# Starting addresses of the supports, the attention output and the transposed x3 in a four-block graph kernel

## The chip, the cores and the metric

The kernel runs on one core of a Trainium2 chip. The metric is the device time of one execution in microseconds, and the figure given is the median of three runs. The engines are named as the profile names them: PE is TensorE (its matmuls), PEld is TensorE's loading of the stationary operand, DVE is VectorE, ACT is ScalarE, POOL is GpSimd and SP is SyncE, which issues the transfers.

## The reference

There are 32 graphs of 256 nodes with 256 features, and a 256 x 256 weighted adjacency each. Every graph passes four blocks, each a residual with a layer norm behind it:

```
x = layernorm(x + relu([x, adj@x / deg] @ W.T))                        # block 0
x = layernorm(x + gcn3(x))          # h = relu(adj@(x@W1)+b1); h = relu(adj@(h@W2)+b2); adj@(h@W3)+b3
x = layernorm(x + attention(x))     # 8 heads of 64, softmax*0.33 + 0.33*adj + 0.33*exp(-adj), then @W_out + b_out
x = layernorm(x + gate(x))          # w = softmax over nodes of sum_m(q@k.T * adj)/8, times v
```

All is float32, and the results are float32.

## The kernel before

The work is written out by hand for each engine, with semaphores between them. One graph takes 340 matmul records on PE, and in the steady part a `slot(s)` runs steps of up to six graphs in turn: the gate of an old one, the attention of a younger one, the three graph-convolution layers of the next, block 0 of the newest. The slots are the loop around everything that the change touches. Nothing but the order of calls in `slot` sets the order on an engine.

**Split products.** To keep float32 precision, every operand of the big products is held as two float32r tiles, a high part (suffix `_h`, written by ACT with `copy`, line 378) and a low part (suffix `_l`, the rest, written by DVE, line 830). A product then takes three passes: high x high, low x high, high x low. `product` (line 1478 holds its matmul) runs them, and each matmul has its own load of a 128 x 128 stationary block (`left`); the moving operand (`right`) is 256, 384 or 512 columns wide. So each matmul is a pair: a weight load of 128 columns from one SBUF address, and a stream of columns from another. The load for the next pair is done while the present one streams. In the profile's names, `psum<-A,B` has the moving operand A first and the stationary B second.

**Steps around the change**, by the names of the tiles:
- The supports `sup` (x times W, before the adjacency is applied). In `hidden` (layers 0 and 1) `sup` is stationary and the adjacency `adjT` is moving; in `gcn_out` and `aggregate` it is the other way round. Each of the four has 12 matmuls of 256 columns per graph.
- `project_out`: `oT`, the attention output, is stationary, and `wout` is moving: 24 matmuls of 256 columns.
- `tail_project`: `x3T` is stationary, `w3` is moving: 12 matmuls of 384 columns.
- `tail_adj_k`: the adjacency is stationary and `k3` (in the profile `k`) is moving, 128 or 64 columns: 8 matmuls.

**Where the tiles lie.** Tiles are allocated in the order of their declarations, each from the next multiple of 32 bytes. Nearly all of them are multiples of 128 bytes long, so a position modulo 128 bytes is carried on from tile to tile, and the little tiles named `space_0`, `space_1` and `space_2` (and the tail `HALF` in the rows of `qkT`) only shift what comes behind them. Every block that a matmul reads starts a multiple of 128 bytes behind its tile's start (in `qkT` a multiple of 64), so the position of the tile is that of all its blocks. Before the change, modulo 128: all weights (`w0`, `w123`, `wqkv`, `wout`, `w3`) at 32; `adjT`, `fT`, `hidT`, `x2T`, `oT`, `x3T`, `k3`, `v_sb`, `x1`, `x2`, `x3` at 96; `sup` at 32; `ident` at 64; `work` at 0. So the stationary and the moving operand of every split product are 64 bytes apart, but for `k3` and the adjacency, which are 0 apart.

Of the kernel before, what the change touches and what calls it, by code (L numbers as in the profile page):

```python
# [7 lines left out]
F32R = mybir.dt.float32r  # L8
# [5 lines left out]
def graph_blocks_kernel(nc, x, adj, nodemask, xT, adjT_in, L0_WT, L1_W1, L1_b1, L1_W2, L1_b2, L1_W3, L1_b3,  # L14
                        L2_Wqkv, L2_Wout, L2_bout, L3_WT, out):
    G, N, F = x.shape
    P = 128
    NT = N // P
# [11 lines left out]
    HALF = 16  # L30
# [7 lines left out]
    with ctx:  # L38
        def sb(name, shape, dt=F32):
            return ctx.enter_context(nc.sbuf_tensor(name, shape, dt))  # L40
# [45 lines left out]
        adjT = [sb(f"adjT_{s}", [P, ADJS, NT, N], F32R) for s in "hl"]  # L86
        fT = [sb(f"fT_{s}", [P, FT, N], F32R) for s in "hl"]

        sb("space_0", [P, HALF])
        sup = [sb(f"sup_{s}", [P, NT, F], F32R) for s in "hl"]  # L90
        sb("space_1", [P, HALF])
        self_part = sb("self_part", [P, NT, F])
        x1_pre = sb("x1_pre", [P, NT, F])
        x1 = sb("x1", [P, NT, F])
# [14 lines left out]
        psum_exp = sb("psum_exp", [P, 2, 2, NT])  # L109
        rsum = sb("rsum", [P, 2, 2, NT])  # L110
        probT = work[:, 1].rearrange("p (a h j i) -> p a h j i", a=2, h=2, j=NT)
        sb("space_2", [P, HALF // 2])
        oT = [sb(f"oT_{s}", [P, PAIRS, N], F32R) for s in "hl"]
        x3_pre = sb("x3_pre", [P, NT, F])
        x3 = sb("x3", [P, NT, F])
# [47 lines left out]
        def bank(n):  # L163
            return psum[:, n]
# [44 lines left out]
        def once(g):  # L209
            return min(g + 1, G)  # L210

        def nth(g, p):
            return min(PAIRS * g + p + 1, PAIRS * G)

        def nth2(g, p, i):
            return min(2 * (PAIRS * g + p) + i + 1, 2 * PAIRS * G)

        def live(g):
            return 0 <= g < G
# [4 lines left out]
        def reuse(eng, semaphore, n):  # L224

            if n > 0:
                eng.wait_ge(semaphore, n)
# [1237 lines left out]
        def _(pe):  # L1465
# [9 lines left out]
            def product(dst, terms, passes=ALL, opens=True, closes=True):  # L1475
                steps = [(left[a], right[b]) for left, right in terms for a, b in passes]
                for n, (left, right) in enumerate(steps):
                    last = mm(dst, left, right, start=opens and n == 0, stop=closes and n == len(steps) - 1)  # L1478
                return last

            def cut(parts, *index):
                return [a[index] for a in parts]
# [3 lines left out]
            def block_of(i, size=P):  # L1486
                return slice(i * size, (i + 1) * size)

            def transpose_tiles(dst, src):
                for r in range(2):  # L1490
                    for t in range(2):
                        last = nc.tensor.transpose(dst[:, r * N + t * P:r * N + (t + 1) * P],  # L1492
                                                   src[:, t, block_of(r)], ident[:, :])
                return last
# [14 lines left out]
            def weights(g, number):  # L1509
                if g == 0:  # L1510
                    pe.wait_ge(dve_w, number)
# [135 lines left out]
            def qk(g, p):  # L1647
                if not live(g):
                    return
                weights(g, W_QKV + 1)  # L1650
                pe.wait_ge(dve_x2T, once(g))
                if p in (2, 3):
                    reuse(pe, act_oT, nth(g - 1, p))
                    reuse(pe, dve_oT, nth(g - 1, p))
                if p == 1:
                    reuse(pe, dve_oT, nth(g - 1, p - 1))
                if p == 0:
                    pe.wait_ge(act_x2T, once(g))
                if p == 3:
                    pe.wait_ge(dve_sup0, once(g + 2))  # L1660
                    pe.wait_ge(act_sup0, once(g + 2))
                for i in range(2):
                    last = product(bank(QK[p])[:, i * N:(i + 1) * N],
                                   [(cut(wqkv, A, k, i, block_of(p)), cut(x2T, A, k)) for k in range(FT)])
                last.then_inc(pe_qk, 1)
# [23 lines left out]
            def probs_t(g, p, h):  # L1689
                if not live(g):  # L1690
                    return
                if (p, h, g) == (0, 0, 31):
                    pe.wait_ge(dve_prob, nth2(g, 0, 0))
                else:
                    pe.wait_ge(dve_prob, nth2(g, p, h))
                    if p == 0 and h == 1:
                        pe.wait_ge(dve_qk, nth(g, p + 2))
                        pe.wait_ge(act_qk, nth(g, p + 2))
                    if p == 1 and h == 1:
                        pe.wait_ge(act_probT, nth2(g, p - 1, 0))  # L1700
                    if p == 2 and h == 1:
                        pe.wait_ge(act_qk, nth(g + 1, p - 2))
                        pe.wait_ge(dve_qk, nth(g + 1, p - 2))
                    if p == 0 and h == 0:
                        pe.wait_ge(act_v, once(g))
                    if p == 3 and h == 1:
                        reuse(pe, act_qkv3, once(g - 1))
                transpose_tiles(bank(PROBT[p][h]), prob[:, p % 2, :, h]).then_inc(pe_probT, 1)
# [79 lines left out]
            def gate_column(g):  # L1788
                if not live(g):
                    return  # L1790
                pe.wait_ge(dve_gate_prob, once(g))
                pe.wait_ge(dve_x2_pre, once(g + 3))
                pe.wait_ge(act_gate_exp, once(g))
                for t in range(NT):
                    last = nc.tensor.transpose(bank(GATE_COL)[:, t:t + 1], gate_prob[:, block_of(t)], one[:, :])  # L1795
                last.then_inc(pe_gate_col, 1)

            def slot(s):
                hidden(0, s - 2, HI)
                tail_adj_k(s - 5)  # L1800
                hidden(0, s - 2, LO)
                probs_t(s - 4, 2, 0)
                probs_t(s - 4, 2, 1)
                probs_t(s - 4, 3, 0)
                probs_t(s - 4, 3, 1)
                scores(s - 3, 0)
# [4 lines left out]
                support(1, s - 2, HI)  # L1811
                support(1, s - 2, LO)
                qk(s - 3, 2)
                support0(s - 1, HI)
                hidden(1, s - 2, HI)
# [11 lines left out]
                aggregate(s - 1, HI)  # L1827
                aggregate(s - 1, LO)
                qk(s - 3, 3)
                gate_column(s - 5)  # L1830
                probs_t(s - 3, 0, 0)
                probs_t(s - 3, 0, 1)
# [7 lines left out]
                x3_transpose(s - 4)  # L1840
                x1_transpose(s - 1)
                qk(s - 2, 0)
                tail_project(s - 4, HI)
                support(0, s - 1, HI)
# [124 lines left out]
            def last_graphs():  # L1969
# [24 lines left out]
                values(G - 2, LO)  # L1994
                qk(G - 2, 3)
                gate_column(G - 4)
                probs_t(G - 2, 0, 0)
                probs_t(G - 2, 0, 1)
# [24 lines left out]
                project_out(G - 2, HI)  # L2023
                project_out(G - 2, LO)
                gate_column(G - 3)
                probs_t(G - 1, 0, 0)
                probs_t(G - 1, 0, 1)
# [70 lines left out]
```

## Time and profile before

| | us |
|---|---|
| median of 3 runs | 1299.63 (1298.72 to 1299.93) |
| the profiled execution, its own time | 1296.4 |
| its span | 1294.6 |
| PE busy / share of span | 1276.8 / 99% |
| DVE busy / share of span | 1198.8 / 93% |
| ACT busy / share of span | 912.2 / 70% |

The busy time of PE counts every moment in which some matmul is under way. A matmul of 256 columns stands in the trace with about 280 ns, but the next one starts about 115 ns after it; what a matmul costs a busy PE is this distance between starts, and it is read from the timeline as the difference between the start of one row and that of a later one, divided by the matmuls between them. The time outside the span is 1.8 us in the profiled execution.

### The profile page before, as it was taken

The page shows a single profiled execution, that of the slowest core. Times are in us where ns is not written, and L with a number is a line of the kernel's source. Part 1 is how long each engine was busy: PE and PEld are TensorE (multiplying, and loading weights), DVE is VectorE, ACT ScalarE, POOL GpSimd, SP SyncE. Part 2 cuts the span into 40 slices and gives each one's busy share as a digit, 9 for nine tenths or more (in the row PEclk, how much of TensorE's full clock was granted, in tenths as well). Part 3 has the DMA queues.
Part 4 walks back from the last instruction along what each step waited for, and adds up shares of the span by engine and source line. Part 5 has one row for each costly group of instructions (what it writes and reads, how often), then busy time and mean ns, then how long its engine had stood idle before and what let it go on. Part 6 is the DMA issues. An engine that isn't in the chain of part 4 may idle for free.

```text
span 1294.6 us, 30579 instructions
## 1 busy us (share of the span) xinstructions
PE 1276.8 (99%) x10987; PEld 1173.4 (91%) x10987; DVE 1198.8 (93%) x3821; ACT 912.2 (70%) x2445; POOL 139.7 (11%) x265
## 2 busy tenths in 40 slices
PE   8999999999999999999999999999999999999997
PEld 7899999999999999999999999999999999999985
DVE  6898999999999999999999999999999999998996
ACT  6677767677667677677677676776676776776773
POOL 0000110101110101111101101011101011110011
PEclk9999999999999999999999999999999999999999
DMA  5211011110111110111100111101111101110000
GB/s 193 68 35 35 1 44 43 43 43 2 43 43 43 43 36 8 43 43 43 43 20 25 44 43 43 43 2 43 43 43 43 35 10 43 43 43 10 9 10 25
DMA packets 51588, 49.03 MB, mean 38 GB/s; under 512 B 7920, under 2 KB 51184, under 8 KB 51440
## 3 DMA queue, kind: packets, MB, share of 16 engines
q1 hardware_dynamic: 51440, 47.08, 11.7%
q8 instruction: 90, 1.47, 0.5%
q14 instruction: 58, 0.48, 0.1%
HBM read 38.68 MB, written 8.39 MB: 36 GB/s over the span
## 4 chain that ended last, share of the span: by engine, by line
PE 96%; DVE 1%; ACT 1%; DMA 1%; issue 0%; POOL 0%; SPq 0%; POOLq 0%; DVEq 0%; ACTq 0%
PE psum L1478 63%; PE psum L1492 13%; PE psum L1722 9%; PE psum L1684 8%; PE psum L1773 1%; PE psum L1776 1%; DMA adj_sb<-in_adj 1%; PE psum L1785 1%; PE psum L1795 0%; POOL rstd L338 0%; ACT fT_h L378 0%; DVE bn L859 0%; SPq L238 0%; DVE x L893 0%; ACT adj_junk L434 0%
## 5 line engine op out<-in xcount | busy, mean ns | idle before, releaser
L526 ACT ACTIVATE work<-work,shift 128x256 f32<-128x256 f32 x512 | 253.6, 499 | 35.9 <-DVE shift L1022 35.9
L1041 DVE SCALAR_TENSOR_TENSOR work<-work,rsum,extra 128x256 f32<-128x256 f32 x512 | 216.4, 472 | 0.2
L378 ACT ACTIVATE work<-psum 128x512 f32<-128x512 f32 x256 | 138.2, 595 | 76.1 <-PE psum L1492 72.2
L1022 DVE CUSTOM_DVE_ANT_0 work<-psum,minus_big 128x256 f32<-128x256 f32 x512 | 189.3, 415 | 0.7 <-PE psum L1684 0.7
L378 ACT ACTIVATE sup_h<-psum 128x512 fp32r<-128x512 f32 x128 | 75.9, 593 | 148.0 <-PE psum L1478 148.0
L335 POOL TENSOR_TENSOR mv<-mv,eps 128x2 f32<-128x2 f32 x128 | 33.0, 258 | 1140.8 <-DVE mv L880 1140.8
L1478 PE MATMUL psum<-x2T_h,wqkv_h 128*128 128x256 f32 x512 | 145.3, 284 | 0.0
L1478 PE MATMUL psum<-x2T_l,wqkv_h 128*128 128x256 f32 x512 | 142.2, 278 | 0.0
L1478 PE MATMUL psum<-x2T_h,wqkv_l 128*128 128x256 f32 x512 | 142.1, 278 | 0.0
L1492 PE MATMUL psum<-ident,work 128*128 128x128 f32 x1024 | 129.3, 274 | 0.0
L1722 PE MATMUL psum<-work,v_sb 128*64 128x256 f32 x1024 | 124.6, 385 | 0.0
L1492 PEld LDWEIGHTS psum<-ident,work 128*128 128x128 f32 x1024 | 112.8, 141 | 1.3 <-issue 0.4
L378 ACT ACTIVATE qkT_h<-psum 128x512 fp32r<-128x512 f32 x128 | 75.5, 591 | 50.9 <-PE psum L1478 50.9
L338 POOL TENSOR_TENSOR rstd<-mv,minus_half 128x2 f32<-128x2 f32 x128 | 107.0, 836 | 10.0
L1722 PEld LDWEIGHTS psum<-work,v_sb 128*64 128x64 f32 x1024 | 67.8, 136 | 36.5 <-issue 0.2
L526 ACT ACTIVATION_READ_ACCUMULATOR work<-work,shift 128x1 f32 x512 | 97.2, 190 | 0.0
L1478 PE MATMUL psum<-w_h,fT_h 128*128 128x256 f32 x384 | 93.7, 280 | 3.2 <-ACT fT_h L378 2.1
L1478 PEld LDWEIGHTS psum<-x2T_l,wqkv_h 128*128 128x128 f32 x512 | 96.7, 189 | 0.1
L1478 PEld LDWEIGHTS psum<-x2T_h,wqkv_h 128*128 128x128 f32 x512 | 96.2, 188 | 0.5 <-issue 0.2
L1478 PEld LDWEIGHTS psum<-x2T_h,wqkv_l 128*128 128x128 f32 x512 | 96.1, 188 | 0.0
L859 DVE BATCH_NORM_STATS2 bn<-x_pre 128x6 f32<-128x256 f32 x256 | 94.5, 410 | 0.2
L1478 PE MATMUL psum<-w_l,fT_h 128*128 128x256 f32 x384 | 93.1, 278 | 0.0
(134 smaller groups left out, 3735.2 us busy)
## 6 DMA issues: line engine op xcount, KB each, us to landing
xT_sb<-in_xT SPq DMA_DIRECT2D x32, 256.0 KB, 2.8
adjT_sb<-in_adjT SPq DMA_DIRECT2D x32, 256.0 KB, 3.2
adj_sb<-in_adj SPq DMA_DIRECT2D x32, 256.0 KB, 4.7
x_sb<-in_x SPq DMA_DIRECT2D x32, 256.0 KB, 4.9
out<-y_sb SPq DMA_DIRECT2D x32, 256.0 KB, 4.6
work<-in_L_gnn_W_qkv SPq DMA_DIRECT2D x1, 1536.0 KB, 9.6
mask_row<-in_nodemask SPq DMA_DIRECT2D x32, 32.0 KB, 4.6
w_raw<-in_L_gnn_W SPq DMA_DIRECT2D x3, 256.0 KB, 6.7
```

What stands on the lines that cost most here:

```text
L335: nc.gpsimd.tensor_tensor(mv[:, k, :, 1], mv[:, k, :, 1], eps[:, :], ALU.add) \
L338: nc.gpsimd.tensor_tensor(rstd[:, k], mv[:, k, :, 1], minus_half[:, :], ALU.pow) \
L378: return nc.scalar.activation(dst, src, ACT.Copy, scale=scale)
L526: last = nc.scalar.activation(prob[:, p % 2, i, h], prob[:, p % 2, i, h], ACT.Exp, bias=shift[:, p % 2, h, i:i + 1], scale=-1.0, accum_out ...
L859: last = V_.bn_stats(out=bn[:, k, t], in_=src[:, t])
L1022: last = V_.tensor_tensor_reduce(out=prob[:, p % 2, i, h], in0=bank(SCORES[p] + h)[:, i * N:(i + 1) * N], in1=minus_big[:, g % 2, i], scal ...
L1041: last = V_.scalar_tensor_tensor(out=prob[:, p % 2, i, h], in0=prob[:, p % 2, i, h], scalar=rsum[:, p % 2, h, i:i + 1], in1=extra[:, g % 2 ...
L1478: last = mm(dst, left, right, start=opens and n == 0, stop=closes and n == len(steps) - 1)
L1492: last = nc.tensor.transpose(dst[:, r * N + t * P:r * N + (t + 1) * P], src[:, t, block_of(r)], ident[:, :])
L1684: last = mm(bank(SCORES[p] + h)[:, i * N:(i + 1) * N], qkT[left][rows, p % 2, 0, block_of(i)], qkT[right][rows, p % 2, 1], start=n == 0 an ...
L1722: last = mm(bank(PV[p])[h * D:(h + 1) * D, 0:N], v_sb[:, k, (2 * p + h) * D:(2 * p + h + 1) * D], probT[:, p % 2, h, k], start=k == 0, sto ...
L1773: mm(bank(ADJK)[:, at:at + 2 * D], adjT[0][:, g % ADJS, k, block_of(t)], k3[:, k].rearrange("p a d -> p (a d)"), start=k == 0, stop=False)
```

## The change

It alters where four groups of tiles start, and nothing of what is computed or in which order:
- `space_0` shrinks from 64 to 32 bytes, each support tile gets 16 bytes of padding at its start, and `space_1` shrinks likewise. `sup_h` then starts at 16 modulo 128 and `sup_l` at 48, where both were at 32. Against `adjT` at 96 they are 48 and 80 bytes apart, where both were 64. All from `self_part` on stays where it was.
- `space_2` grows from 32 to 64 bytes. All tiles behind it move on by 32 bytes: `oT`, `x3_pre`, `x3`, `x3T`, `qkv3`, `k3`, `gate` go from 96 to 0 modulo 128, and the small tiles, `x4_pre`, `y_sb`, `bn`, `mv` and `rstd` with them. `oT` and `x3T` are then 96 bytes behind their weights (which are at 32) where they were 64, and the adjacency 96 behind `k3` where it was 0.
- At three places two of PE's waits for semaphores that stand next to each other (in the third with one between) change places. The same semaphores and values are waited for before the same matmul.

```diff
-        sb("space_0", [P, HALF])
-        sup = [sb(f"sup_{s}", [P, NT, F], F32R) for s in "hl"]
-        sb("space_1", [P, HALF])
+        sb("space_0", [P, 8])
+        sup = [sb(f"sup_{s}", [P, 4 + NT * F], F32R)[:, 4:].rearrange("p (t f) -> p t f", t=NT) for s in "hl"]
+        sb("space_1", [P, 8])
...
-        sb("space_2", [P, HALF // 2])
+        sb("space_2", [P, 16])
         oT = [sb(f"oT_{s}", [P, PAIRS, N], F32R) for s in "hl"]
...
                 if p == 3:
+                    pe.wait_ge(act_sup0, once(g + 2))
                     pe.wait_ge(dve_sup0, once(g + 2))
-                    pe.wait_ge(act_sup0, once(g + 2))
...
                     if p == 0 and h == 1:
+                        pe.wait_ge(act_qk, nth(g, p + 2))
                         pe.wait_ge(dve_qk, nth(g, p + 2))
-                        pe.wait_ge(act_qk, nth(g, p + 2))
...
                 pe.wait_ge(dve_gate_prob, once(g))
+                pe.wait_ge(act_gate_exp, once(g))
                 pe.wait_ge(dve_x2_pre, once(g + 3))
-                pe.wait_ge(act_gate_exp, once(g))
```

Every engine's list of instructions, without its waits, is the same before and after.

## Rows read from the trace of the kernel before

**Rows 1.** Page: span, busy time and share of each engine, granted clock
```profile
span 1294.6 us, 30579 instructions
...
PE 1276.8 (99%) x10987; PEld 1173.4 (91%) x10987; DVE 1198.8 (93%) x3821; ACT 912.2 (70%) x2445; POOL 139.7 (11%) x265
...
PEclk9999999999999999999999999999999999999999
```
**Rows 2.** Page: the chain that ended last, by engine
```profile
PE 96%; DVE 1%; ACT 1%; DMA 1%; issue 0%; POOL 0%; SPq 0%; POOLq 0%; DVEq 0%; ACTq 0%
```
**Rows 3.** Windows of one slot each: busy us of each engine, records, clock, transfers
```profile
605.00:644.28 39.28, 39.28 (x342) 36.26 (x342) 37.10 (x121) 28.19 (x77) 4.38 (x8) 1.00 0.12 35
900.00:939.28 39.28, 39.28 (x345) 36.25 (x343) 37.10 (x120) 28.19 (x77) 4.38 (x8) 1.00 0.12 36
```
**Rows 4.** PE's waits: for whom, us in total, times, longest
```profile
PE psum L1478 <- ACT sup_h L378: 2.5, 5, 1.1
...
PE psum L1478 <- ACT x3T_h L378: 0.4, 1, 0.4
```
**Rows 5.** Timeline of PE, 590 to 604 us: start, us, operation, count
```profile
591.58 0.28 PE L1478 MATMUL psum<-w_h,fT_h 128*128 128x256 f32 x1
...
592.52 0.28 PE L1478 MATMUL psum<-adjT_h,sup_h 128*128 128x256 f32 x1
...
593.94 0.63 PE L1478 MATMUL psum<-w_h,fT_l 128*128 128x256 f32 x4
...
595.77 0.28 PE L1478 MATMUL psum<-wout_h,oT_h 128*128 128x256 f32 x1
...
598.49 0.28 PE L1478 MATMUL psum<-w_h,hidT_h 128*128 128x256 f32 x1
...
599.85 0.39 PE L1478 MATMUL psum<-wqkv_h,x2T_h 128*128 128x512 f32 x1
...
601.68 0.28 PE L1478 MATMUL psum<-sup_h,adjT_h 128*128 128x256 f32 x1
...
603.04 1.10 PE L1478 MATMUL psum<-wqkv_h,x2T_l 128*128 128x512 f32 x4
```
**Rows 6.** The same timeline, 604 to 619 us
```profile
604.12 0.28 PE L1478 MATMUL psum<-sup_h,adjT_l 128*128 128x256 f32 x1
...
605.41 0.28 PE L1478 MATMUL psum<-x2T_h,wqkv_h 128*128 128x256 f32 x1
...
615.45 0.34 PE L1478 MATMUL psum<-w_l,x3T_h 128*128 128x384 f32 x1
...
616.69 0.28 PE L1478 MATMUL psum<-w_h,fT_h 128*128 128x256 f32 x1
...
618.07 0.85 PE L1478 MATMUL psum<-w_h,x3T_l 128*128 128x384 f32 x4
618.76 0.28 PE L1478 MATMUL psum<-x2T_h,wqkv_h 128*128 128x256 f32 x1
```
**Rows 7.** The same timeline, 620 to 624 us
```profile
620.17 0.28 PE L1478 MATMUL psum<-adjT_h,sup_h 128*128 128x256 f32 x1
...
621.12 0.34 PE L1773 MATMUL psum<-k,adjT_h 128*128 128x128 f32 x2
...
621.93 0.72 PE L1478 MATMUL psum<-adjT_h,sup_l 128*128 128x256 f32 x4
622.49 1.91 PE L1492 MATMUL psum<-ident,work 128*128 128x128 f32 x16
```
**Rows 8.** Page: a group by line: count, busy us, mean ns, idle before
```profile
L1492 PE MATMUL psum<-ident,work 128*128 128x128 f32 x1024 | 129.3, 274 | 0.0
```
**Rows 9.** Groups of DVE by line: count, busy us, mean ns, idle before
```profile
L830 DVE TENSOR_TENSOR sup_l<-psum,sup_h 128x512 fp32r<-128x512 f32 x128 | 87.4, 682 | 2.4 <-ACT sup_h L378 2.4
...
L830 DVE TENSOR_TENSOR x2T_l<-psum,x2T_h 128x512 fp32r<-128x512 f32 x32 | 21.8, 682 | 0.0
```

## The prediction

> **What bounds the kernel now.** I read the page's first part first. PE is busy for 99% of the span, DVE for 93%, and PE's clock is granted in full, so at the higher of its levels, 2.4 GHz, all the way [rows 1]. The chain of waits says the same: 96% of it is PE, with no other engine over 1% [rows 2]. The windows of two steady slots, each 39.28 us, show PE busy for all 39.28 us and DVE for 37.10 [rows 3]. PE's waits are a few in the whole run: 2.5 us in all for the supports' high part, 0.4 for x3 transposed [rows 4]. So the end is set by how closely matmuls follow each other on PE. Whatever shortens that is gained until DVE is full, which is 39.28 - 37.10 = 2.18 us per graph away; whatever lengthens it is lost in full, times 32 graphs.
>
> The timeline of PE then shows what the change can reach. The distance between two starts of the same kind of matmul isn't one number. With 256 columns moving it has two levels:
> - The attention's output projection: 595.77 to 598.49 us, 2.72 us for 24 matmuls, 113.3 ns each. The third layer's support behind it (to 599.85, 12 matmuls) and the third layer's adjacency product (601.68 to 603.04, 12 matmuls) also go at 1.36 / 12 = 113.3 ns [rows 5].
> - The second layer's adjacency product: 592.52 to 593.94, 12 matmuls, 118.3 ns; the eight before it, of another tile, 0.94 / 8 = 117.5 ns [rows 5]. Block 0's `aggregate`, from its second matmul: 604.12 to 605.41, 11 matmuls, 117.3 ns [rows 6]. The first layer's, 620.17 to 621.12, 8 matmuls, 118.8 ns; its low part, 621.93 to 622.49, 4 in 0.56 us, with one long start among them [rows 7].
>
> The same operation at the same distance of 64 bytes therefore runs at 113.3 or near 118, and holds its level over a dozen matmuls and over a change of tile. A lower level also exists: 16 transposes fill 1.91 us, and one lasts 0.27 us by the page, so (1.91 - 0.27) / 15 = 109.3 ns from start to start [rows 7, 8]. A transpose moves half the columns but loads the same 128 columns of stationary operand, so 109.3 ns looks like the weight load alone, 113.3 like the load and the stream disturbing each other a little, and 118 like more of that. That reading of the levels is mine; the trace shows the numbers only.
>
> **The change part by part.** It adds and removes no instruction. What can change is this distance, in four places, and in those that come directly behind them.
>
> *Supports, 64 to 48 and 80 bytes from the adjacency* (48 matmuls per graph). I assume that at the new distances they run at the better of the two levels seen today. Then `hidden` of layer 1 saves 1.42 - 12 x 0.1133 = 0.06 us, `aggregate` 11 x (117.3 - 113.3) = 0.044, `hidden` of layer 0 0.95 - 8 x 0.1133 = 0.043 in its high part and, with 0.36 us left for three matmuls if the long start is 0.2 us, about 0.02 in its low part; `gcn_out` saves nothing, it is at 113.3 already. Sum 0.167 us per graph. The bounds: at 109.3 ns throughout it would be 0.108 + 0.088 + 0.076 + 0.03 + 0.05 (`gcn_out`) = 0.35 us per graph; at 118.3 throughout, `gcn_out` loses 12 x 5 = 0.06 and `aggregate` 0.01.
>
> *`oT`, 64 to 96 bytes behind `wout`* (24 matmuls). It is at the good level now [rows 5], so on this assumption nothing. Bounds: to 109.3 saves 24 x 4 = 0.096 us; to 118.3 costs 24 x 5 = 0.12.
>
> *`x3T`, 64 to 96 behind `w3`* (12 matmuls of 384 columns). The high part has 1.24 / 7 = 177.1 ns per matmul, the low part 0.69 / 4 = 172.5 [rows 6]. Again at the better of the two: 7 x 4.6 = 0.032 us. Lower bound by the transposes' rate with 384/256 of the stream, 164 ns: 7 x 13 + 4 x 8.5 = 0.125 saved. Upper bound: the low part at 177.1 too, 0.018 lost.
>
> *`k3`, from 0 to 96 bytes between it and the adjacency* (8 small matmuls, 0.81 us from the first to the next step [rows 7]). These are as long as their weight loads, a few ns above the transposes' 109.3 at most. I take 0; bounds 0.02 either way.
>
> *The waits that change places.* Both stay before the same matmul, and the trace has waits of PE for neither the pair at `qk` nor that at the transposes. 0; a wait that is checked in another order could cost a few ns on each of three places, so 0.02 us per graph either way.
>
> *DVE and ACT on the moved tiles.* DVE makes `sup_l` (at 32 modulo 128) in 682 ns and `x2T_l` (at 96) in 682 [rows 9], so a move by 32 or 64 bytes shows nothing. A start at 16 modulo 32 isn't in the trace. Even a few per cent more on 128 such operations would fit in DVE's 2.18 us of slack. 0.
>
> *What follows.* A level is carried over to the next step: the third support and the 512-column products behind it inherit the good level from `oT` today. If `oT` falls to 118 these 12 matmuls lose another 12 x 5 = 0.06 us. This belongs to the upper bound.
>
> Sum: 0.167 + 0.032 = 0.20 us per graph, x 32 = 6.4 us; a faster PE will wait a little more for ACT's high parts, which it already does now and then [rows 4], and I take a fifth of it off: 5 us. The profiled execution (1296.4 us, span 1294.6) would come to 1291.4; the median of the runs is 3.2 us above it, so 1299.6 - 5 = **1294.6 us**. Bounds: all to the lowest level, (0.35 + 0.096 + 0.125 + 0.02) x 32 = 18.9 us saved, 1280.7; all to the highest, (0.07 + 0.12 + 0.018 + 0.06 + 0.04) x 32 = 9.9 us lost, 1309.5.
>
> **The rivals.**
>
> *A. Position does nothing (no change, 1299.6).* For it: the same distance of 64 bytes gives both levels, and which one holds changes at the borders of steps [rows 5, 6]. That could be a rhythm between loads and streams set by how a step begins, in which the address has no part. Against it: inside a long run the level is steady to a nanosecond while ACT and DVE work all the time, so the disturbance comes from PE's own two reads, and these have an address each. The Trainium skill speaks for this rival: "SBUF — State Buffer", section "Who interferes with whom", gives PE two independent read ports, one for the moving operand and one for the weight load, and says that PE never waits on anyone; by it the addresses would change nothing, 1299.6. The skill's "TensorE: Matmul & The Clock Gate" (section "Wait — 56ns, not 53.3ns?") puts back-to-back matmuls at columns / 2.4 GHz and 2.5 ns, 109.2 for 256 columns. The trace doesn't agree with that figure: the split products stand at 113.3 and 118 [rows 5, 6].
>
> *B. The lowest level.* At 48, 80 and 96 bytes loads and streams miss each other altogether, and all four groups go to 109.3 ns. For it: the transposes, with the same 128-column weight loads, reach it [rows 7, 8], so the loads allow it. Against it: no 256-column split product of the rows does, and the transposes' streams are half as long. 18.9 us saved, of which DVE's slack (2.18 us against 0.59 per graph) takes nothing: 1281, or 1284 with the same fifth lost.
>
> *C. Slower.* 64 bytes is the farthest that two positions modulo 128 can be apart. 48, 80 and 96 are all nearer (48, 48 and 32 going the short way round). If nearness is what hurts, `oT` and `gcn_out`, which run at 113.3 today, fall to 118.3, and the third support with them: (0.06 + 0.12 + 0.06) x 32 = 7.7 us lost, and `x3T` 0.6 more, 1308; with `oT` alone it is 0.12 x 32 = 3.8, 1303.4. For it: `k3`, 0 bytes from the adjacency, stands right between products at 118.8 and a slow start [rows 7]. It decides as soon as the output projection leaves 113.3 ns.
>
> **How the numbers follow.** A measurement of this kernel tells about 0.2% from no change, 2.6 us. Forecast (supports and `x3T` at their better level): 0.38. A, no change: 0.22. B, or a good part of it: 0.16. C: 0.24. Faster by over 0.2% is the forecast and B, 0.54; within 0.2% is A, 0.22; slower 0.24. Range: B reaches to 1281 and C to 1308; with a tenth left out at either end, 1285 to 1304. The forecast's own range is 1290 to 1297.
>
> **What would show it.** In PE's timeline: `hidden` of layer 1 as 12 matmuls in 1.36 us, not 1.42; `aggregate` as 11 in 1.25; the seven high-part matmuls of `tail_project` in 1.21; the output projection still at 2.72 for 24. B would show 1.31, and 2.62 for the output projection; C 1.42 for `gcn_out` and 2.84 for the output projection. A steady slot would be 39.1 us for the forecast, 38.7 for B, 39.5 for C. It would be wrong if steps that the change doesn't touch (`qk`, `values`, the support products) change their level: then the rhythm is handed on from step to step, and no sum by touched steps can hold. It would also be wrong if DVE's time per operation on `sup_l` left 682 ns.

## The result and the profile after

The changed kernel takes 1307.49 us (median of 6 runs, 1305.1 to 1309.02) beside 1298.26 us for the kernel before (6 runs, 1296.55 to 1299.93): ratio 1.0069, 95% interval 1.0057 to 1.008. It is 9.2 us slower, where 5 us faster was forecast. The profiled execution takes 1307.15 us.

The page of the changed kernel, in the lines of [rows 1] and [rows 2]: the same number of instructions, the full clock, and 11.3 us more of busy PE.

```profile
span 1305.4 us, 30579 instructions
...
PE 1288.1 (99%) x10987; PEld 1184.9 (91%) x10987; DVE 1202.3 (92%) x3821; ACT 912.9 (70%) x2445; POOL 139.7 (11%) x265
...
PEclk9999999999999999999999999999999999999999
...
PE 96%; DVE 1%; DMA 1%; ACT 1%; issue 0%; POOL 0%; SPq 0%; POOLq 0%; DVEq 0%; ACTq 0%
```

One slot in a window, columns as in [rows 3] (900 to 939.57 us reads the same). A slot is 39.57 us long, where it was 39.28; 0.29 x 32 graphs = 9.2 us is the whole difference. PE is busy in every moment of it, and DVE still has 2.36 us left.

```profile
605.00:644.57 39.57, 39.57 (x343) 36.55 (x342) 37.21 (x121) 28.22 (x76) 4.38 (x8) 1.00 0.13 36
```

PE's waits (for whom; us in total, times, longest) are if anything fewer than in [rows 4]: 1.4 us for the supports' high part, where it was 2.5. So no wait was added; matmuls follow each other more slowly.

```profile
PE psum L1478 <- ACT sup_h L378: 1.4, 4, 0.4
```

PE's timeline after, with the rows that answer to [rows 5] (start, us, operation, count):

```profile
598.38 0.29 PE L1478 MATMUL psum<-adjT_h,sup_h 128*128 128x256 f32 x1
...
599.81 0.64 PE L1478 MATMUL psum<-w_h,fT_l 128*128 128x256 f32 x4
...
601.65 0.28 PE L1478 MATMUL psum<-wout_h,oT_h 128*128 128x256 f32 x1
...
604.53 0.28 PE L1478 MATMUL psum<-w_h,hidT_h 128*128 128x256 f32 x1
...
605.89 0.39 PE L1478 MATMUL psum<-wqkv_h,x2T_h 128*128 128x512 f32 x1
...
607.73 0.28 PE L1478 MATMUL psum<-sup_h,adjT_h 128*128 128x256 f32 x1
...
609.14 1.09 PE L1478 MATMUL psum<-wqkv_h,x2T_l 128*128 128x512 f32 x4
```

`hidden` of layer 1 (from `adjT_h,sup_h`): 1.43 / 12 = 119.2 ns, where [rows 5] had 118.3. The output projection: 2.88 / 24 = 120.0, where it was 113.3. The third support behind it: 1.36 / 12 = 113.3, as before, so the slow projection is not handed on. `gcn_out`: 1.41 / 12 = 117.5, where it was 113.3.

Farther on in the same timeline, the rows that answer to [rows 6, 7]:

```profile
610.22 0.28 PE L1478 MATMUL psum<-sup_h,adjT_l 128*128 128x256 f32 x1
...
611.53 0.29 PE L1478 MATMUL psum<-x2T_h,wqkv_h 128*128 128x256 f32 x1
...
619.90 0.36 PE L1478 MATMUL psum<-x2T_h,wqkv_h 128*128 128x256 f32 x1
...
621.40 0.37 PE L1478 MATMUL psum<-w_h,x3T_h 128*128 128x384 f32 x1
621.60 0.34 PE L1478 MATMUL psum<-w_l,x3T_h 128*128 128x384 f32 x1
...
622.82 0.28 PE L1478 MATMUL psum<-w_h,fT_h 128*128 128x256 f32 x1
...
624.20 0.87 PE L1478 MATMUL psum<-w_h,x3T_l 128*128 128x384 f32 x4
624.90 0.28 PE L1478 MATMUL psum<-x2T_h,wqkv_h 128*128 128x256 f32 x1
...
626.32 0.28 PE L1478 MATMUL psum<-adjT_h,sup_h 128*128 128x256 f32 x1
...
627.26 0.34 PE L1773 MATMUL psum<-k,adjT_h 128*128 128x128 f32 x2
```

`aggregate`: 1.31 / 11 = 119.1 ns, where it was 117.3. `qk` of pair 0, whose operands were not moved: 1.50 us for 12 matmuls. The high part of `tail_project` behind its first start: 1.22 / 7 = 174.3 (it was 177.1); its low part 0.70 / 4 = 175 (172.5). `hidden` of layer 0: 0.94 / 8 = 117.5 (118.8).

To see where the 0.287 us of a slot lie I took, for every step, the time from its start to the start of the next as a median over 28 steady slots, from the timelines of both kernels and of the experiments. The steps that differ, in ns per slot (e1 and e2 are the first two experiments):

| step | operands moved by the change | before | after | e1 | e2 |
|---|---|---|---|---|---|
| project_out | oT | 2720 | 2882 | 2883 | 2720 |
| gcn_out | sup | 1362 | 1416 | 1362 | 1416 |
| hidden, layer 1 | sup | 1412 | 1432 | 1412 | 1432 |
| aggregate | sup | 1434 | 1452 | 1442 | 1453 |
| tail_project, high part | x3T | 1478 | 1421 | 1422 | 1478 |
| tail_project, low part | x3T | 691 | 704 | 704 | 691 |
| qk of pair 0 | none | 1458 | 1499 | 1498 | 1458 |
| qk of pair 3 | none | 1455 | 1484 | 1465 | 1484 |
| whole slot | | 39280 | 39567 | 39446 | 39400 |

### The profile page after: what moved, and what is told of

Same layout as the page of the kernel before. It is cut to its first block, busy times and chain, and to the rows that moved or that the text cites. A ratio compares the mean times of both kernels' runs of the same rounds, so it can differ in the third digit from the quotient of the medians.

```text
span 1305.4 us, 30579 instructions
## 1 busy us (share of the span) xinstructions
PE 1288.1 (99%) x10987; PEld 1184.9 (91%) x10987; DVE 1202.3 (92%) x3821; ACT 912.9 (70%) x2445; POOL 139.7 (11%) x265
## 4 chain that ended last, share of the span: by engine, by line
PE 96%; DVE 1%; DMA 1%; ACT 1%; issue 0%; POOL 0%; SPq 0%; POOLq 0%; DVEq 0%; ACTq 0%
PE psum L1478 63%; PE psum L1492 13%; PE psum L1722 9%; PE psum L1684 8%; PE psum L1773 1%; PE psum L1776 1%; DMA adj_sb<-in_adj 1%; PE psum L1785 1%; PE psum L1795 0%; POOL rstd L338 0%; ACT fT_h L378 0%; DVE bn L859 0%; SPq L238 0%; DVE x L893 0%; ACT adj_junk L434 0%
```

## Experiments on the parts of the change

The theory after the result was: the distance sets the level directly, `oT` at 96 costs most and the supports the rest, and the swapped waits cost nothing. The rivals were that the swapped waits do it, and that something that all three parts share (how steps hand on a rhythm) does, so that the parts would not add up.

**e1: the tiles behind `space_2` alone** (5 runs).

```diff
-        sb("space_2", [P, HALF // 2])
+        sb("space_2", [P, 16])
```

> Only the tiles behind space_2 move by 32 bytes (oT, x3T, k3 and what lies behind them); supports and waits are as before. Theory D (each pair of operands has a level of its own, set by its distance): the output projection goes from 113.3 to 120.3 ns per matmul as in the changed kernel, 24 x 7 x 32 = 5.4 us, and the whole is 5 to 6.5 us slower than before. Rival R (the distance has no level of its own; any small shift of the start of a step tips a rhythm that is handed on): the output projection may stay at 113.3, steps that no address touches change, and the time can fall anywhere from before to the changed kernel's.

Measured: 1302.85 us beside 1299.21, ratio 1.0033 (1.0021 to 1.0046): 4.3 us slower, a little less than expected.

**e2: the supports alone** (9 runs): the three lines `space_0`, `sup`, `space_1` of the change.

> Only the supports move, to 48 and 80 bytes from the adjacency; oT, x3T and the waits are as before. D: the third layer's adjacency product goes from 113.3 to about 118 ns, the others stay near 118, and the steps right behind them lose a little: 3 to 4.5 us slower than before, and this and the run with only oT and x3T moved add up to the changed kernel's 9.2 us. R: they do not add up.

Measured: 1301.59 us beside 1299.21, ratio 1.0022 (1.0013 to 1.0032).

**e3: the three swaps of waits alone** (11 runs), as in the change's last three pieces.

> Only the three pairs of waits change places; every address is as before. D: no change, within 1 us of before. R: a wait seen some ns earlier or later can tip the rhythm as well, so up to several us either way.

Measured: 1298.61 us, ratio 0.9998 (0.9989 to 1.0007). The slot is 39.280 us, as before. One slot in windows, first of e1, then of e2:

```profile
605.00:644.45 39.45, 39.45 (x342) 36.42 (x341) 37.17 (x120) 28.21 (x77) 4.38 (x8) 1.00 0.11 35
```

```profile
605.00:644.40 39.40, 39.40 (x342) 36.38 (x341) 37.13 (x120) 28.22 (x77) 4.38 (x8) 1.00 0.12 37
```

+0.166 and +0.120 us per slot make 0.286, and the whole change has 0.287. So by the slots of one execution each the parts add up, the larger costs are found again in their own part (table), and the waits are nothing. The times of whole runs say it less sharply: 0.33% and 0.22% make 0.55%, beside 0.69% for the whole, which their intervals allow. The rise of `qk` of pair 0 belongs to e1, that of `qk` of pair 3 mostly to e2: steps that were not moved changed behind steps that were. The 8 to 10 ns of `aggregate` and `qk` of pair 3 in e1 are not e1's: the runs v1, v2, v3 and v6 below, which move no tile, have them too.

**e4 and e5: `oT` and the tiles from `x3_pre` on, apart.** Both add a tile `space_3` right behind `oT`; e4 (8 runs) has `oT` 96 bytes behind `wout` and `x3T` back at 64 modulo 128, e5 (10 runs) the other way round. Modulo 256, though, e4 does not put the tiles behind `oT` back: its two spaces are 128 bytes longer than before, so `x3T` is 192 bytes behind `w3` where it was 64.

```diff
+++ e4
-        sb("space_2", [P, HALF // 2])
+        sb("space_2", [P, 16])
         oT = ...
+        sb("space_3", [P, 24])
+++ e5
         oT = ...
+        sb("space_3", [P, 8])
```

> Only oT moves (96 bytes behind wout); a space behind it puts x3, x3T, k3 and gate back at 96 modulo 128. Theory D (a pair's level comes from its distance, and steps hand on only what follows from it): the output projection at 2.88 us per graph for its 24 matmuls instead of 2.72, all other steps as before, a steady slot about 39.44 us, 5 us slower. The alternative, that the tiles further back cause part of it: the slot of 39.446 us of the run that moved all of them is not reached, and qk of pair 0 (1.458 us before, 1.498 there) tells whose it was.

> The rest of that: oT stays at 64 bytes, x3, x3T, k3 and gate move by 32. D: the first tail product's high part gains as its level falls from 177 to 173 ns, its low part loses 0.013 us, and qk of pair 0, which no moved operand touches but which runs right behind the transposes of x3 and x1 and before the tail product, goes from 1.458 to 1.498 us because it is tipped to its upper level; the slot within 0.01 us of before's 39.28, the time within 1 us.

Measured, beside 1299.22: e4 1302.35 us, ratio 1.0025 (1.0015 to 1.0036), slot 39.407; e5 1297.82 us, ratio 0.9993 (0.9984 to 1.0003), slot 39.274. In e4 the projection rises by 0.163 us, and the high part of `tail_project` gives 0.034 back. That step was expected to stay; `x3T` had moved by 128 bytes, and whether that did it was not separated. In e5 that part falls by 0.057, its low part rises by 0.013, the high part of layer 0's `hidden` falls by 0.013, and `qk` of pair 0 rises by 0.041: a gain and a loss that nearly cancel. So, step by step, the loss of e1 is `oT`. The slots do not add up, +0.127 and -0.006 beside e1's +0.166, and most of what is missing is the 0.034 of `tail_project`.

**e6: `oT` at 0 bytes from `wout`** (one run). `space_2` 24 and `space_3` 16 elements. Nearness modulo 128, rival C's mechanism, makes this the worst of all distances. Modulo 256 `oT` is 128 bytes from `wout` here, and the tiles behind it lie as in e4.

> oT at 32 modulo 128, 0 bytes from wout; all else as before. If nearness is what costs, the output projection is slower than at 96 bytes (32 the short way round): over 120.1 ns per matmul, 2.9 us or more for 24. If 64 bytes is one good point among equals, it is again about 120. If position does nothing, 113.3.

Measured: 1303.46 us, one run, beside 1299.22. PE's timeline of e6 (the matmul stands in line 1479 here):

```profile
599.41 0.28 PE L1479 MATMUL psum<-wout_h,oT_h 128*128 128x256 f32 x1
...
602.25 0.28 PE L1479 MATMUL psum<-w_h,hidT_h 128*128 128x256 f32 x1
...
603.66 0.40 PE L1479 MATMUL psum<-wqkv_h,x2T_h 128*128 128x512 f32 x1
```

The projection has 2.84 / 24 = 118.3 ns, less than the 120.0 at 96 bytes. In the step itself the nearer position is not the slower one. But the level is now handed on: the third support behind it has 1.41 us for 12, 117.5 ns, and by the step medians it rises from 1360 to 1417 ns and `gcn_out` from 1362 to 1415, though neither's operands moved. At 96 bytes the projection is slower (120.0) and the support behind it stays at 113.3. In the whole slot 0 bytes costs more: 39.480 us, +0.200, where e4 has +0.127. So this run does not decide on nearness.

## Experiments on the distance by itself

**m1: pairs of weight load and matmul alone** (one run). It computes nothing of the reference. One moving tile at 0 modulo 128 (`mv`) and eight stationary tiles 0, 16, ... 112 bytes behind it (their names in Roman numerals). Groups of 24 matmuls of 256 columns, first with four transposes between the groups, again with a moving tile 32 bytes farther on (`mv_shift`), then with `mv` and without transposes, up and down; also 384, 512 and 128 columns. ACT and DVE are idle, and the clock is granted in full from 20 to 228 us. The code, shortened:

```python
for n in range(24):
    matmul(psum[:, bank, 0:256], st[d][:, (n % 3) * 128:(n % 3 + 1) * 128],
           moving[:, (n % 2) * 256:(n % 2) * 256 + 256], start=n == 0, stop=n == 23)
```

> A kernel of its own that computes nothing of the reference (it copies x to the output): after loading, only PE works. It runs groups of 24 matmuls, each with its own 128-column weight load, with the stationary operand 0, 16, ... 112 bytes behind the moving one (modulo 128): separated by transposes, with both operands moved by 32 bytes, then without separation up and down, then with 384, 512 and 128 columns. D: the ns per matmul depend on the distance, 113 at 64 bytes, about 120 at 96, and moving both operands by 32 bytes changes nothing. R: all distances of separated groups have the same level, and in the unseparated part the level depends on what ran before. A third possibility, that ACT and DVE cause the extra 4 to 11 ns: then all groups here stand at 109 ns, since both are idle.

PE's timeline of m1, groups behind transposes, then groups directly behind each other:

```profile
20.46 3.12 PE L76 MATMUL psum<-mv,st_zero 128*128 128x256 f32 x24
23.41 0.60 PE L69 MATMUL psum<-ident 128*128 128x128 f32 x4
...
33.63 2.99 PE L76 MATMUL psum<-mv,st_lxiv 128*128 128x256 f32 x24
36.45 0.60 PE L69 MATMUL psum<-ident 128*128 128x128 f32 x4
...
40.06 3.07 PE L76 MATMUL psum<-mv,st_xcvi 128*128 128x256 f32 x24
42.96 0.60 PE L69 MATMUL psum<-ident 128*128 128x128 f32 x4
...
66.24 3.07 PE L76 MATMUL psum<-mv_shift,st_xcvi 128*128 128x256 f32 x24
69.15 0.60 PE L69 MATMUL psum<-ident 128*128 128x128 f32 x4
...
84.26 2.99 PE L76 MATMUL psum<-mv,st_lxiv 128*128 128x256 f32 x24
87.08 2.97 PE L76 MATMUL psum<-mv,st_lxxx 128*128 128x256 f32 x24
...
104.10 2.89 PE L76 MATMUL psum<-mv,st_lxiv 128*128 128x256 f32 x24
106.83 1.34 PE L76 MATMUL psum<-mv,st_xlviii 128*128 128x256 f32 x10
```

Behind transposes the group at 0 takes 2.95 us, at 64 2.82, at 96 2.90. Without transposes ahead the same tile pair at 64 takes 2.82 us on the way up (117.5 ns each) and 2.73 on the way down (113.8). The steady levels with `mv`, from the single starts: 0: 120, 16: 120 or 118.3, 32: 118, 48: 118, 64: 113.3 or 117.8, 80: 116.8, 96: 117.3 or 119, 112: 117.2, or 117 and 123 in turn. So the two levels of [rows 5, 6] exist without any other engine, only 64 bytes has the better of them, and no distance goes below 113.3.

The distance modulo 128 is not all that counts. With `mv_shift` the levels at the same distances are 0: 118.2, 16: 118.8, 32: 120.0, 48: 118.3, 64: 117.8 (2.91 us, the row of `st_xcvi`), 80: 118.8, 96: 117.1, 112: 117.6: no group is at 113, and 32 bytes is now slower than 0. So moving both operands by 32 bytes did change something, against the theory that this distance sets the level. Modulo 256 each of these groups is also 128 bytes farther apart than its like with `mv`, so the absolute position and the distance modulo 256 are not told apart here; m3 below compares 64 and 192. With 128 columns every distance shows the same, here 0 (24 matmuls):

```profile
203.66 2.88 PE L76 MATMUL psum<-mv,st_zero 128*128 128x128 f32 x24
```

By the single starts that is 111.7 ns, the shortest spacing of a float32r pair in this trace. With 384 columns it was 173.3 at 0, 32, 48, 64 and 96, 175.6 at 80, and 177 at 16 and 112; with 512, 226.7 at 0 and 112, 230.0 at 48 and 233 to 234 elsewhere.

The Trainium skill says in "SBUF — State Buffer", section "Who interferes with whom", that PE's two read ports are independent and that PE waits on no one. Rival A read it to mean that addresses change nothing. This trace does not agree with that reading, and the measurement decides: with DVE and ACT idle the same matmuls take 113 to 120 ns by where the two operands lie.

**m2: what tips the level at 64** (one run). It computes nothing of the reference. Groups of 24 at 64, ahead of them 1 to 6 transposes; then one, then twelve matmuls at another distance. Shortened:

```python
for turn in range(6):
    level(mv, 64, 24); transposes(1 + turn)
for d in others:
    level(mv, d, 1); level(mv, 64, 24)
```

> Matmuls alone, nothing of the reference computed (x is copied to the output). Groups of 24 at 64 bytes behind 1 to 6 transposes, at two absolute positions (moving operand at 0 and at 32 modulo 128); then 24 at 64 bytes behind one matmul at another distance, and behind twelve of them. If the two levels of 64 bytes (113.3 and 117.7) are states that a step inherits, both occur, each is held to the end of its group, and the one matmul before decides which. If the absolute position decides, all groups of one position have one level. If chance decides, groups of the same kind differ.

PE's timeline of m2:

```profile
22.95 0.27 PE L94 MATMUL psum<-ident 128*128 128x128 f32 x1
22.98 3.08 PE L84 MATMUL psum<-mv,st_lxiv 128*128 128x256 f32 x24
25.90 0.38 PE L94 MATMUL psum<-ident 128*128 128x128 f32 x2
...
58.15 0.37 PE L84 MATMUL psum<-mv,st_zero 128*128 128x256 f32 x1
58.36 2.90 PE L84 MATMUL psum<-mv,st_lxiv 128*128 128x256 f32 x24
61.09 0.28 PE L84 MATMUL psum<-mv,st_xvi 128*128 128x256 f32 x1
61.21 2.99 PE L84 MATMUL psum<-mv,st_lxiv 128*128 128x256 f32 x24
64.04 0.28 PE L84 MATMUL psum<-mv,st_xxxii 128*128 128x256 f32 x1
```

Behind one transpose the group at 64 takes 2.92 us, with a first start of about 0.2 us in it: 118.3 ns each. The other five such groups, behind 2 to 5 transposes and behind the run-in, have 2.82 to 2.84 (near 114). With both tiles 32 bytes farther on, still 64 apart, five of six groups have 2.91 or 2.92 and one, behind two transposes, 2.81; behind one matmul at another distance all seven such groups stand at 117.8. With `mv`, a pair at 0 ahead gives 2.73 us (113.8); one at 16 ahead gives 2.83 (117.9), and that is held through four more groups, behind one matmul at 32, 48, 80 and 96; behind one at 112 it is 2.73 again. Neither the number of transposes nor the other distance gave a rule: behind twelve matmuls at 112, 96, 80 and 16 the group is at 113.8, behind twelve at 48, 32 and 0 near 118. Twelve at 96 bytes take 120.0 ns each here, where m1 had 117.3 or 119: not only 64 bytes has several levels.

## Experiments that try to use it

**v1, v2, v3: the order of matmuls inside the products** (one run each): a high-low pass ahead of high x high (v1, `LEFT_LATE` and `RIGHT_LATE`; v3, `ALL`), or the blocks of nodes in these products in reverse (v2).

```diff
+++ v1
-            LEFT_LATE = (((0, 0), (0, 1)), ((1, 0),))
-            RIGHT_LATE = (((0, 0), (1, 0)), ((0, 1),))
+            LEFT_LATE = (((0, 1), (0, 0)), ((1, 0),))
+            RIGHT_LATE = (((1, 0), (0, 0)), ((0, 1),))
+++ v2
-                for t in range(NT):
+                for n, t in enumerate(reversed(range(NT))):
...
+++ v3
-            ALL = ((0, 0), (0, 1), (1, 0))
+            ALL = ((0, 1), (0, 0), (1, 0))
```

> All addresses as before; in the two-part products (supports, adjacency products, block 0) the first two passes change places: high x low comes ahead of high x high. Same matmuls, same distances of 64 bytes. If the level of a step is a state that is handed on from how it begins, some of the steps change between 113.3 and 117.7 ns per matmul, up or down, by up to 0.33 us per graph in all (75 matmuls by 4.4 ns). If the level belongs to the pair of tiles, or to what ACT and DVE do at that time, each step keeps its time within 0.01 us.

> The same question: only the two blocks of 128 nodes in these products are taken in reverse order. Same expectations: some steps change level if it is inherited, none if it belongs to the tiles or to other engines.

> The same question for qk, the output projection and the scores: their pass order becomes high x low, high x high, low x high. If the level is inherited, the output projection and what follows it may leave 113.3, or qk of pair 1 may leave 118; if not, all stay within 0.01 us.

Measured: 1296.22, 1298.38 and 1300.25 us, one run each, beside 1298.22. No step changed between the two levels; the slots are 39.254 to 39.260 us. The 0.02 us below before lie in the support of layer 0 (1381 ns before, 1363 to 1364 in v1 and v2) and the high part of `tail_project` (1478 and 1458 to 1459), and v6 below has them too, so they are not the order's: in these steps, and in `aggregate` and `qk` of pair 3, differences of 8 to 20 ns come without any tile being moved. All blocks and both parts of an operand lie at one position modulo 128, so another order leaves the sequence of distances as it was.

**v4: moving operands on one side, stationary ones on the other** (8 runs). Small tiles of 64 bytes put `w0`, `w123`, `wout`, `w3` and `adjT` at 96, and `fT`, `hidT`, `oT`, `x3T` and the supports at 32: every split product 64 apart, as before, with the moving operand at 96 and the stationary one at 32. Three steps are the other way round: `values`, `aggregate` and `gcn_out`.

```diff
+        sb("space_a", [P, HALF])      # ahead of w0; likewise b (wqkv), c (wout), d (mask_all_u8),
+        ...                           # e (fT), f and g (around hidT), h (behind oT), i and j (around x3T)
-        sb("space_0", [P, HALF])
-        sb("space_2", [P, HALF // 2])
+        sb("space_2", [P, HALF + HALF // 2])
```

> Waits and order as before; w0, w123, wout and w3 go from 32 to 96 modulo 128, fT, hidT, oT and x3T from 96 to 32. Every pair stays 64 bytes apart, but now most borders between steps are 64 apart too (the next step's first weight load against the last step's moving operand), where before they were 0 at seven of them: second support to qk of pair 2, that to block 0's support, that to the second adjacency product and that to its low part and on, tail product to qk of pair 1 and more. If an encounter at 0 bytes at a border is what tips a step from 113.3 to 117.7 ns, then block 0's support and the second adjacency product fall from 118 to 113 (24 matmuls, 0.1 us per graph), and with qk of pair 1 and the first adjacency product it may be 0.2 us: 39.05 to 39.2 us per slot, 3 to 7 us faster. If borders don't matter, the slot stays within 0.03 us of 39.28.

Measured: 1302.03 us beside 1298.90, slower where faster was expected: ratio 1.0023 (1.0012 to 1.0034), slot 39.373. `support` of layer 1, `qk` of pair 2, `support0` and layer 1's `hidden` reach 113 ns (0.16 us won in the four), but from one longer start of 154 ns at the low part of block 0's support on, the steps up to `gcn_out` stand near 118 in the median.

**v5: the same with DVE's `gate_probs(s - 6)` moved behind `x_lo(s - 2)`** (11 runs, one of which took 1801.39 us), and **v6, that move alone** (one run). If the longer start, a wait for DVE's `fT_l`, is what tips the level, taking it away holds 113 through the projection.

```diff
-                gate_probs(s - 6)
...
                 x_lo(s - 2)
+                gate_probs(s - 6)
```

> The exchanged positions, and on DVE gate_probs (0.35 us) one place of three calls later, so that scores, the low part of the second support and fT_l come 0.35 us earlier. If the wait for fT_l tips the level: block 0's low part goes back from 0.51 to 0.453 us, the output projection from 2.83 to 2.72, the third support from 1.416 to 1.36, and a slot is 39.1 us or less, 4 to 7 us faster than before. If the addresses tip it, the output projection stays at 2.83 and the slot at 39.3 or more.

> Addresses as before, and only gate_probs moved on DVE. Before has no wait at that place, so nothing is to be gained: the steps from the second support to the third adjacency product keep their times within 0.01 us, the slot within 0.03 of 39.28.

Measured: v5 1300.97 us beside 1298.68, ratio 1.0016 (1.0007 to 1.0026), slot 39.334; v6 1297.09 us, one run beside 1298.68, slot 39.253. PE's timeline of v5:

```profile
597.28 0.28 PE L1487 MATMUL psum<-adjT_h,sup_h 128*128 128x256 f32 x1
...
600.46 0.28 PE L1487 MATMUL psum<-wout_h,oT_h 128*128 128x256 f32 x1
...
603.28 0.28 PE L1487 MATMUL psum<-w_h,hidT_h 128*128 128x256 f32 x1
```

The longer start is gone, and 28 matmuls from 597.28 to 600.46 go at 113.6 ns. The projection still has 2.82 / 24 = 117.5, from its first matmul on. The wait as the cause is refuted: the level falls at the change of tiles.

Over all slots that border changes the level both ways. In v5 24 slots reach it at 113 and run the projection at 117.8 (2.83 us), and 4 reach it at 118 and run it at 113.3 after six matmuls (2.74 us, the first from 364.36 us on). In v4 it is 16 and 11 slots, and one that stays at 118. Modulo 256 both operands take a step of 128 bytes at this border, the weights from 96 to 224 and the activations from 160 to 32, while their distance is 64 on either side.

**v7: v5 with 128 more bytes at six places** (5 runs): `space_c`, `d`, `f`, `g`, `h` of 3 x `HALF` and `space_2` of 3 x `HALF` + `HALF` / 2. The distances are then alike modulo 256 too: but for `values`, `aggregate` and `gcn_out`, the moving operand is at 96 and the stationary one at 160. At the border into the projection neither operand takes a step.

> As the run with exchanged positions and the earlier fT_l, but wout, hidT and oT moved by another 128 bytes, so that the stationary operand is 64 behind the moving one modulo 256 in every left product, borders between steps included, up to the third support. If a step of 128 bytes at a border tips the level: the output projection returns to 2.72 us (24 x 113.3 ns), the third support to 1.36, a slot near 39.1, 4 us or more faster than before. If only positions modulo 128 count (and something else tips it there), the projection stays at 2.83.

Measured: 1292.33 us (1291.62 to 1295.35, 5 runs) beside 1299.11: ratio 0.9948 (0.9934 to 0.9962). It beats both kernels. PE's timeline of v7, and one slot in a window:

```profile
594.79 0.28 PE L1487 MATMUL psum<-adjT_h,sup_h 128*128 128x256 f32 x1
...
597.97 0.28 PE L1487 MATMUL psum<-wout_h,oT_h 128*128 128x256 f32 x1
...
600.69 0.28 PE L1487 MATMUL psum<-w_h,hidT_h 128*128 128x256 f32 x1
```

```profile
605.00:644.04 39.04, 39.04 (x342) 36.02 (x342) 36.95 (x120) 28.08 (x76) 4.38 (x8) 1.00 0.12 37
```

From 594.79 to 600.69 there are 52 matmuls in 5.90 us, 113.5 ns, the projection (2.72 / 24) among them; so it is in all 28 steady slots. The slot is 39.04 us, and 0.24 x 32 = 7.7 us of gain is expected where 6.8 is measured. By the step medians `hidden` of layer 1 and `qk` of pair 1 each stand 52 ns below before, `support` of layer 1 39 and `support0` 35. `gcn_out` and `aggregate`, where the adjacency is stationary and the support moves, so that the distance is 192 modulo 256, stay near 118 (1415 and 1441 ns).

**m3: does a step of 128 bytes tip the level?** (one run). It computes nothing of the reference. Moving at 128 modulo 256, stationary 64 (`near`) or 192 (`far`) behind it.

> Matmuls alone again (x is copied to the output). Groups of 24 with the stationary operand 64 (near) or 192 (far) bytes behind modulo 256, in turn, and one matmul of the other kind within a group. If 128 bytes matter, the level changes at the borders of groups or at the single one; if not, each chain keeps the level in which it begins (113.3 or 117.7 ns) over all its groups.

PE's timeline of m3, from the round behind three transposes and from the one behind four:

```profile
32.46 2.88 PE L88 MATMUL psum<-mv,st_far 128*128 128x256 f32 x24
35.18 2.88 PE L88 MATMUL psum<-mv,st_near 128*128 128x256 f32 x24
...
44.00 2.99 PE L88 MATMUL psum<-mv,st_far 128*128 128x256 f32 x24
46.83 2.88 PE L88 MATMUL psum<-mv,st_near 128*128 128x256 f32 x24
```

Both distances show both levels: `far` 2.72 us (113.3) at 32.46, and 2.83 (117.9) at 44.00. At 113 the border from near to far and back tips nothing, eight times. At 118 it sometimes does, so neither expected outcome came out clean: `near` behind `far` comes back to 113.3 (46.83 us; also at 23.81), and so does `far` behind a single `near` (three times), while at eight other borders 118 is kept. So 64 and 192 are alike in themselves, and a step between them was never enough to lose the level, but five times went with winning it back. Here only the stationary operand takes the step; a step of both, as v5 has it at the projection, was not tried alone. Why v5 loses the level there and v7 does not stays open.

## Why the prediction was wrong

**What held.** PE sets the end, matmul spacing is the only thing the change can reach, DVE has room, and whatever a step gains or loses comes out in full: 0.287 us x 32 = 9.2 us against 9.2 measured. The waits were worth 0 (e3). `k3`'s step (`tail_adj_k`) was put at 0 and has 812 ns before and after. DVE's time on `sup_l` stayed (683 ns in the median before, 684 after).

**The step that failed** is "I assume that at the new distances they run at the better of the two levels seen today". It made 64 bytes the place where an operand could be unlucky, and every other distance a place where it could not. It is the other way round. In m1, with the moving operand at 0, only 64 bytes reaches 113.3 at all; at 48, 80 and 96 the same pairs have 118, 116.8 and at least 117.3. So steps near 118 had next to nothing to win, and those at 113.3 everything to lose:
- Supports: forecast -0.167 us per graph. Measured `hidden` of layer 1 +0.020, `aggregate` +0.018, `gcn_out` +0.054, `hidden` of layer 0 +0.001: +0.093. The working's upper bound was 0.07.
- `oT`: forecast 0, bound +0.12. Measured +0.162, since 96 bytes gives 120.0 ns in the kernel (as in m2) and not 118.3. This is over half of the loss, and it exceeds the bound because the bound was taken from the highest level of the rows, at another distance.
- `x3T`: forecast -0.032; the seven intervals of the high part gave 0.02 and the low part lost 0.013. The first start of the step is 40 ns shorter, and `qk` of pair 0 ahead of it 41 longer, so that border is worth nothing; why it moved I can't say.
- Steps not touched: forecast nothing but the third support, which in fact stayed. `qk` of pairs 0 and 3 rose by 0.070 together. The prediction named this as what would make it wrong.

**The rivals.** *A, position does nothing*, is refuted by e1 and e2, where only tiles were moved. Half of it holds: at 64 bytes the same pair has two levels, and in m1 and m2 what ran before, not the address, chooses between them. *B, the lowest level*, is refuted by m1: 113.3 is the best at 256 columns, 111.7 even at 128, so 109.3 from the transposes was no bound for these pairs. *C, slower*, gave 1308, 8.3 us lost, for 9.2 measured, and its deciding sign came true: the output projection left 113.3, and `gcn_out` rose as it said (1.41 us for 1.42). The third support did not fall, and the sum matches by luck: `oT` cost more, and the untouched steps something, where that support cost nothing. Nearness as the mechanism is not shown. For it: with `mv` in m1 64 bytes, the farthest, is the best and 0 the slowest, and 0 bytes costs the kernel more per slot than 96 (e6). Against it: with `mv_shift` 32 bytes (120.0) is slower than 0 (118.2), and the projection itself is faster at 0 bytes (118.3) than at 96 (120.0).

**What stays open.** What chooses between 113.3 and 118 at 64 bytes; no experiment gives a rule, v7 shows one arrangement that holds. What v7's gain comes from, since 128 bytes were added in six places at once. For the projection it is not the distance modulo 256, which is 64 in v5 and in v7; the absolute position and the step at the border into it remain. The prediction and most experiments count modulo 128, which no run showed to be the period. Why `gcn_out` stands at 118 in v4, v5 and v7. That loads and streams disturb each other is the likeliest reading of m1, and only argued.

## What to carry to other kernels

Where PE is busy all the time, measure the spacing of starts by step, not the length of a matmul, and treat a step at the best level as something that a new address can only lose. Two levels at one distance don't prove that the distance is bad: time the pair alone before moving tiles, which takes one small kernel, and at the positions of the kernel itself, since the distance modulo 128 alone did not give the level. A space that restores a tile modulo 128 can still move it by 128 bytes: count modulo 256 too. When an arrangement is changed, read the steps behind it too, since a level is carried over to operands that were not moved.

## What the runs showed of the hardware that I had not expected

- Where the stationary and the moving operand lie changes the spacing of 256-column float32r matmuls with no other engine at work: with the moving one at 0 modulo 128, 113.3 or 117.8 ns at a distance of 64, 116.8 at 80, 120 at 0; with it at 32, 118.2 at 0 and 120.0 at 32 (m1).
- At 64 bytes the level is a state: it holds over 52 matmuls and two changes of product (v7), one matmul at another distance ahead can set it (m2), and a border between products can change it both ways (v5: 24 slots from 113 to 118, 4 from 118 to 113).
- A level is handed on to a step whose operands were not moved: with `oT` at 0 bytes the third support rose from 1360 to 1417 ns (e6).
- At 128 columns the distance doesn't matter, 111.7 ns at all eight (m1).
- The order of the distances is not the same at every width: at 512 columns 0 and 112 are the best (226.7 ns) and 64 is among the slow ones (233) (m1).
